# Conv, Fourier mixing, attention and routed block on one core: keys in two halves around the channel DFT, counts behind the second up product, batch 0's first taps on ScalarE, another order in the drain

## The chip, the cores and the metric

The kernel runs on one core of one Trainium2 chip. The metric is the time of one launch in device microseconds. The core has a tensor engine (TensorE, PE in the profile; its weight loads are PEld), VectorE (DVE), ScalarE (ACT), GpSimd (POOL) and SyncE (SP), which here only issues transfers. Each engine works through its own list of instructions in order; semaphores tie the lists together.

## The reference, cut to what matters

The input x has 8 batches of 750 frames with 192 channels. Per batch:

```python
h = depthwise_conv(x, 7 taps) + b_dw            # 750 frames, 192 channels
h = relu(w_pw @ h + b_pw); h = max over pairs   # 375 tokens, 192 channels
y = real(fft2(h))                               # DFT over tokens, then over channels
h = layernorm(y) * gamma + beta                 # "spectrum"
h = h + token_statistics_attention(layernorm(h))     # w_qkv, softmax over tokens, w_out
z = layernorm(h); n = layernorm(z) * g1 + b1
scores = sigmoid(n @ Wr + br)                   # the 56 tokens with the lowest scores
attn = softmax attention (12 heads) for these tokens; mix = (n + scores * pooled) @ Wm + bm
hh = z + where(selected, attn @ Wo + bo, mix)
out = h + hh + gelu(layernorm(hh) @ W1 + bf1) @ W2 + bf2
```

## The kernel before

**Three batches in flight.** Each engine has a function `step(p, q, r, w)`, and `pipeline` calls it in the same order on all of them: batch p in front (convolution, both DFTs, first attention), batch q in the middle (routing and second attention), batch r last (the up and down products of the forward block), and w is the batch whose depthwise sums are made ahead. The steps are (0, -, -), called alone; (1, 0, -), the second step; six full steps from (2, 1, 0) to (7, 6, 5); the drain (-, 7, 6); and the forward block of batch 7 by itself. The order inside a step is written out by hand for each engine, so where an instruction stands in one engine's `step` decides what waits behind it.

**Front batch.** `depthwise` multiplies the frames by a tap and adds: tap 0 on ScalarE (`first_tap`, L893), taps 1 to 6 on VectorE (L390). Batch 0 has a function of its own, `depthwise_first`: for each third of the frames (250) VectorE makes all seven taps for both halves of the channels (L403 for tap 0, L411 for the others), and TensorE's `pointwise` (L1161, L1162) starts on a third when its sums are there. Then `relu` (ACT L884) and `pool_pairs` (DVE L427), `over_tokens` (PE L1171, the DFT over the tokens), `spectrum_parts` (ACT), `over_channels` (PE L1183, the DFT over the channels; it waits for the values' copies and for `block_mix`, DVE L606), `spectrum_stats` (DVE L440), `spectrum_center`, a power on GpSimd (L834), `spectrum_norm`, a second power, `second_norm` (DVE L471, it makes xh), and `front_input` (PE L1119, transposes of xh), behind which the qkv products run.

**Middle batch.** `routed_input` transposes nr (PE L1112) into two banks of `zb`; ScalarE and VectorE split the result into nT (L952, L590). `values_keys` (PE L1127) makes values and scores, and then the keys in two halves, one into bank 3 and one into bank 2 of `zb`; ScalarE copies each to kT (L967). `score_sums` (PE L1268) spreads the scores over the partitions in bank 3, once the first half of kT is copied. VectorE's `ranks` (from L614) compares them, `ranks` on TensorE (L1275, "the counts") sums the comparisons, `slots` on VectorE (L629) makes putT, `slots` on TensorE (L1283) turns it, and `selected`, `selected_queries` (L1301) and `logits` follow. `unselected_scores` (DVE L634) writes one more row of putT. `third_norm` and `third_norm_end` (DVE L569, L576) make nr; L576 waits for a power on GpSimd.

**Last batch.** `forward_input` transposes n2 (PE L1119) and VectorE's `forward_input` (L477, L478) makes the low parts of n2T. `forward_up(r, j)` makes six up products (L1134 to L1142), two banks in turn, so that from the third on each waits for a gelu of ScalarE (L1026). ScalarE loads the Gelu table ahead of them (`table_hint`, L1044) and the Exp table behind them (L1070).

`idle_products` (PE L1409) are products that nobody reads. A product of plain fp32 operands shows as two matmul passes in the trace. On TensorE the order of the part that matters is

```python
                if last:
                    forward_up(r, 0)
                if drain:
                    pe.wait_ge(*h1_done.of(q))
                    idle_products(xb[:, 0], 3)
                if middle:
                    routed_input(q)
                if front:
                    over_tokens(p)
```

and then `values_keys`, `score_sums`, `over_channels`, up products 1 and 2, `ranks`, up product 3, `slots`, up product 4, `selected`, up product 5, `selected_queries`, `front_input`. In the second step idle products stand where the up products do.

## Time and profile before

| what | value |
|---|---|
| three runs | 561.88, 563.33, 565.0 us; median 563.33 us |
| profiled execution, its own time | 564.93 us |
| its span, first to last instruction | 563.1 us |
| mean granted TensorE clock | 0.97 of full |
| busy: TensorE | 500.4 us, 89% of the span |
| busy: VectorE, ScalarE, GpSimd | 430.4 us (76%), 245.5 us (44%), 68.6 us (12%) |
| from one full step to the next (transposes of xh, 282.00 to 342.68) | 60.7 us |

The profiled execution took 1.6 us longer than the median. Times inside the trace count from its first instruction. The busy time of an engine says little by itself: TensorE waits in some places and runs at half its clock in others, so the chain, the waits in brackets in the timeline and the granted clock by window are read together.

### The profile page before, as it was taken

What the parts mean: (1) busy time and instruction counts of PE and PEld (TensorE: products, weight loads), DVE (VectorE), ACT (ScalarE), POOL (GpSimd) and SP (SyncE); (2) the same over time, 40 slices, a digit from 0 to 9 for tenths busy, and PEclk for the clock granted to TensorE, in tenths of its full rate; (3) what the DMA queues carried; (4) which work ended last, traced back from release to release, by engine and by line L of the source; (5) the groups of instructions that cost most, each with busy time, mean ns of one, the idle gap of its engine ahead of it and who ended that gap; (6) DMA issues with size and microseconds to landing.
All of it is one profiled execution on the core that took longest, in us unless ns stands there. A gap on an engine that the chain in (4) does not pass through costs nothing.

```text
span 563.1 us, 9011 instructions
## 1 busy us (share of the span) xinstructions
PE 500.4 (89%) x3066; PEld 412.5 (73%) x3066; DVE 430.4 (76%) x1266; ACT 245.5 (44%) x625; POOL 68.6 (12%) x67
## 2 busy tenths in 40 slices
PE   1588799889989998999999998999899989978786
PEld 1456478659877987788877896798778887857575
DVE  5777869779978997889878998899788574864350
ACT  0244123542666155814673257426571367214721
POOL 0001011101220122001300121012200130012001
PEclk9998999899999998999989999999899998978998
DMA  8350100010001000100001000100000000000001
GB/s 243 114 149 1 41 2 1 1 42 1 1 2 41 17 6 1 42 2 20 0 0 41 20 0 0 41 20 0 0 0 2 20 0 1 2 21 0 2 11 31
DMA packets 8392, 13.26 MB, mean 24 GB/s; under 512 B 1911, under 2 KB 6834, under 8 KB 8365
## 3 DMA queue, kind: packets, MB, share of 16 engines
q1 hardware_dynamic: 8365, 12.92, 8.2%
q8 instruction: 15, 0.25, 0.2%
q14 instruction: 12, 0.10, 0.1%
HBM read 10.61 MB, written 2.30 MB: 23 GB/s over the span
## 4 chain that ended last, share of the span: by engine, by line
PE 64%; DVE 17%; issue 9%; ACT 5%; POOL 3%; DMA 1%; DVEq 0%; SPq 0%; ACTq 0%; POOLq 0%
PE xb L1231 7%; PE xb L1171 6%; PE zb L1127 6%; PE yb L1393 6%; PE xb L1183 3%; POOL rs L834 3%; PE zb L1333 3%; DVE dw L411 2%; PE zb L1341 2%; PE xb L1161 2%; PE xb L1134 2%; ACT w_sq L931 2%; PE xb L1162 2%; PE xb L1222 2%; DVE junk L532 2%
## 5 line engine op out<-in xcount | busy, mean ns | idle before, releaser
L834 POOL TENSOR_TENSOR rs<-ve,half 125x3 f32<-125x3 f32 (+1 forms) x32 | 33.5, 1047 | 375.6 <-DVE ve L378 315.8
L390 DVE SCALAR_TENSOR_TENSOR dw<-x_in,w_dw_sb,dw 96x750 f32<-96x750 f32 x84 | 78.8, 992 | 0.4
L1231 PE MATMUL xb<-scratch,w_sq 128*125 128x192 f32 x288 | 48.8, 327 | 0.8 <-DVE scratch L549 0.7
L1231 PEld LDWEIGHTS xb<-scratch,w_sq 128*125 128x125 f32 x288 | 46.7, 188 | 2.2 <-DVE scratch L549 1.2
L1393 PE MATMUL yb<-w_sb,gelu 128*125 128x192 f32 x252 | 46.2, 326 | 0.0
L1393 PEld LDWEIGHTS yb<-w_sb,gelu 128*125 128x125 f32 x252 | 41.5, 187 | 0.0
L1171 PE MATMUL xb<-dft_n_sb,pooled_h 125*96 125x376 f32 x96 | 34.6, 514 | 1.0 <-DVE pooled_h L427 0.9
L1020 ACT ACTIVATE n2T<-zb 128x375 fp32r<-128x375 f32 (+1 forms) x16 | 7.7, 481 | 61.1 <-PE zb L1119 60.9
L1026 ACT ACTIVATE gelu<-yb,b_sb 128x375 f32<-128x375 f32 x48 | 27.2, 569 | 11.6 <-PE yb L1142 10.6
L1161 PE MATMUL xb<-w_pw_sb,dw 97*125 97x192 f32 x64 | 18.0, 366 | 14.7 <-DVE dw L411 14.0
L1333 PEld LDWEIGHTS zb<-ident_sb,probs 128*125 128x125 f32 x144 | 19.0, 187 | 14.2 <-issue 10.2
L524 DVE TENSOR_TENSOR w_sq<-w_s,xb 128x376 f32<-128x376 f32 x48 | 25.0, 536 | 5.6 <-PE xb L1222 5.6
L930 ACT ACTIVATE w_s<-xb 128x375 f32<-128x375 f32 x48 | 23.9, 499 | 11.8 <-PE xb L1142 11.8
L1333 PE MATMUL zb<-ident_sb,probs 128*125 128x128 f32 x144 | 24.1, 293 | 5.4 <-ACT probsT L1003 2.8
L1171 PEld LDWEIGHTS xb<-dft_n_sb,pooled_h 125*96 125x96 f32 x96 | 16.0, 173 | 16.1 <-issue 15.0
L1134 PE MATMUL yb<-n2T,w_sb 128*128 128x376 f32 x48 | 20.6, 430 | 5.6 <-DVE n2T L478 3.6
L532 DVE CUSTOM_DVE_ANT_0 junk<-w_sq,w_s 128x375 f32<-128x375 f32 x48 | 25.4, 542 | 0.0
L1134 PE MATMUL xb<-xhT,w_qkv_sb 128*128 128x376 f32 x48 | 21.8, 454 | 3.6 <-ACT w_sq L931 2.9
L942 ACT ACTIVATE scratch<-w_out_sb,natt 128x192 f32<-128x192 f32 x24 | 9.2, 445 | 36.3 <-DVE natt L543 36.3
L1003 ACT ACTIVATE probsT<-zb 125x384 f32<-125x384 f32 x48 | 22.2, 493 | 5.7 <-PE zb L1333 5.7
L1161 PEld LDWEIGHTS xb<-w_pw_sb,dw 97*125 97x125 f32 x64 | 11.9, 209 | 16.7 <-issue 12.7
L931 ACT ACTIVATE w_sq<-xb 128x375 f32<-128x375 f32 x48 | 23.9, 499 | 0.0
(215 smaller groups left out, 1284.4 us busy)
## 6 DMA issues: line engine op xcount, KB each, us to landing
x_in<-in_x SPq DMA_DIRECT2D x8, 567.0 KB, 4.2
out<-res_f SPq DMA_DIRECT2D x7, 281.2 KB
gelu<-in_w_qkv SPq DMA_DIRECT2D x1, 768.0 KB, 6.8
gelu<-in_w SPq DMA_DIRECT2D x1, 768.0 KB, 4.3
w_out_sb<-in_w_out SPq DMA_DIRECT2D x1, 576.0 KB
w_sb<-in_w SPq DMA_DIRECT2D x1, 576.0 KB
rows_sb<-in_rows SPq DMA_DIRECT2D x1, 504.0 KB
dft_n_sb<-in_dft_n SPq DMA_DIRECT2D x1, 493.5 KB
```

The costliest lines, as they stand in the source:

```text
L390: dve.scalar_tensor_tensor(out=dw[0:C, c, :], in0=x_in[:, c, k:k + S], scalar=w_dw[:, c, k:k + 1], in1=dw[0:C, c, :], op0=ALU.mult, op1=AL ...
L532: dve.tensor_tensor_reduce(out=junk[:, j % 2, 0:N], in0=u[:, j, 0:N], in1=w_s[:, j, 0:N], scale=1.0, scalar=0.0, op0=ALU.mult, op1=ALU.add ...
L834: pool.tensor_tensor(out_[:], in_[:], half3[:] if len(in_.shape) == 3 else half3[:, 0, :], ALU.pow).then_inc(rs.sem, 1)
L931: act.activation(w_sq[:, j, 0:N], xb[:, j % 2, 0:N], ACT.Square, accum_out=nrm[:, j:j + 1]).then_inc(sq_done.sem, 1)
L1026: act.activation(gelu[:, j, 0:N], yb[:, j % 2, 0:N], ACT.Gelu, bias=b_1[:, j:j + 1]).then_inc(gelu_done.sem, 1)
L1127: ins = mm(o, a[:, k], b[:, l], start=start and k + l == 0, stop=stop and k == 1)
L1134: mm(o, w[:, 0, cols], x[:, 0, :], start=True, stop=False)
L1161: mm(o, dw[0:C + 1, 0, f0:f0 + 2 * P - 1:2], w_pw[:, 0, :], start=True, stop=False)
L1171: ins = mm(xb[0:C, c, 0:2 * KF], pooled_h[:, t, chan(c)], dft_n[:, t, :], start=(t == 0), stop=(t == T - 1))
L1231: ins = mm(o, u[:, j, tok(t)], w_oa[:, j, :], start=(j == 0), stop=(j == IT - 1))
L1333: ins = pe.transpose(zb[0:P, 2 + j % 2, 128 * t:128 * t + 128], probs[:, j, tok(t)], ident[:])
L1393: ins = mm(o, gelu[:, j, tok(t)], w_2[:, j, :], start=(j == 0), stop=(j == IT - 1))
```

## The change

Five things are moved; no arithmetic is changed.

1. Batch 0's tap 0 goes from VectorE (L403) to ScalarE (`first_taps`), third by third, with a semaphore of its own for the first two thirds.
2. `values_keys` is split into `joined_values` and `keys(b, k)`. Both halves of the keys use bank 2, so the second waits for the copy of the first. On TensorE the order becomes values, first half, `score_sums`, `over_channels`, second half. On ScalarE the second copy to kT stands behind the table hint and `spectrum_sines`, ahead of the gelus.
3. Up product 2 goes from before the counts (`ranks`) to behind them.
4. `unselected_scores` on VectorE goes from behind `front_input` to before `second_norm`.
5. In the last full step VectorE runs `third_norm_end` ahead of `forward_input`. In the drain TensorE runs five idle products in place of three, first of all, and up product 0 goes behind `routed_input`.

```diff
@@ -175,7 +175,7 @@
         pads, highs, lows = signal("pads"), signal("highs"), signal("lows")
         dw_first, dw_done = signal("dw_first", CT), signal("dw_done", CT * (K - 1))
-        dw_part = signal("dw_part", CT * K * (T - 1))
+        dw_part, dw_begun = signal("dw_part", CT * (K - 1) * (T - 1)), signal("dw_begun", CT * (T - 1))
         pw_ready, relu_done, pool_done = signal("pw_ready", T), signal("relu_done", T), signal("pool_done", T)
@@ -395,22 +395,18 @@
                 for t in range(T):
                     last = t == T - 1
+                    sem, base = (dw_done.sem, 0) if last else (dw_part.sem, CT * (K - 1) * t)
                     f0, f1 = 2 * P * t, 2 * P * (t + 1)
-                    for k in range(K):
+                    for k in range(1, K):
                         for c in range(CT):
-                            src, dst = x_in[:, c, k + f0:k + f1], dw[0:C, c, f0:f1]
-                            if k == 0:
-                                ins = dve.tensor_scalar(dst, src, w_dw[:, c, 0:1], w_dw[:, c, K:K + 1], ALU.mult, ALU.add)
+                            if k > 1:
+                                dve.wait_ge(sem, base + CT * (k - 2) + c + 1)
+                            elif last:
+                                dve.wait_ge(*dw_first.of(0, c + 1))
                             else:
-                                if not last:
-                                    dve.wait_ge(dw_part.sem, CT * K * t + CT * (k - 1) + c + 1)
-                                elif k == 1:
-                                    dve.wait_ge(*dw_first.of(0, c + 1))
-                                else:
-                                    dve.wait_ge(*dw_done.of(0, CT * (k - 2) + c + 1))
-                                ins = dve.scalar_tensor_tensor(out=dst, in0=src, scalar=w_dw[:, c, k:k + 1], in1=dst,
-                                                               op0=ALU.mult, op1=ALU.add)
-                            ins.then_inc((dw_first if k == 0 else dw_done).sem if last else dw_part.sem, 1)
+                                dve.wait_ge(dw_begun.sem, CT * t + c + 1)
+                            dve.scalar_tensor_tensor(out=dw[0:C, c, f0:f1], in0=x_in[:, c, k + f0:k + f1], scalar=w_dw[:, c, k:k + 1],
+                                                     in1=dw[0:C, c, f0:f1], op0=ALU.mult, op1=ALU.add).then_inc(sem, 1)
 
@@ -753,14 +749,14 @@
                     spectrum_center(p)
                     spectrum_norm(p)
+                if middle:
+                    unselected_scores(q)
                 if front:
...
                 if front:
                     front_input(p)
-                if middle:
-                    unselected_scores(q)
                 if first(p):
@@ -805,11 +801,13 @@
                 if front:
                     third_norm(p)
+                if ends(p):
+                    third_norm_end(p)
                 if middle:
...
                 if last and middle and not front:
                     result(r, 1)
-                if front:
+                if front and not ends(p):
                     third_norm_end(p)
@@ -893,6 +891,16 @@
                        .then_inc(dw_first.sem, 1)
 
+            def first_taps():
+
+                act.wait_ge(taps_in.sem, 16)
+                act.wait_ge(*x_ready.of(0))
+                for t in range(T):
+                    f0, f1 = 2 * P * t, 2 * P * (t + 1)
+                    for c in range(CT):
+                        act.activation(dw[0:C, c, f0:f1], x_in[:, c, f0:f1], ACT.Identity, scale=w_dw[:, c, 0:1], bias=w_dw[:, c, K:K + 1])\
+                           .then_inc((dw_first if t == T - 1 else dw_begun).sem, 1)
+
             def split_high(k):
@@ -951,7 +959,7 @@
                 act.activation(nT[0:C, 0, :, 0:N], zb[0:C, 0:2, 0:N], ACT.Copy).then_inc(nT_high.sem, 1)
 
-            def values_keys(b):
+            def joined_values(b):
                 for k, (t0, t1) in enumerate(((0, 2), (2, 3))):
@@ -962,9 +970,10 @@
                     src = zb[0:P, 0:2, 0:D] if k == 0 else joined(2)[:, 0:D].unsqueeze(1)
                     act.activation(v[:, t0:t1, :], src, ACT.Copy).then_inc(v_done.sem, 1)
-                for c in range(CT):
-                    act.wait_ge(*k_ready.of(b, c + 1))
-                    act.activation(kT[:, c, 0:N], zb[0:C, 3 - c, 0:N], ACT.Identity, bias=b_k[:, c:c + 1]).then_inc(kT_done.sem, 1)
+
+            def keys(b, c):
+                act.wait_ge(*k_ready.of(b, c + 1))
+                act.activation(kT[:, c, 0:N], zb[0:C, 2, 0:N], ACT.Identity, bias=b_k[:, c:c + 1]).then_inc(kT_done.sem, 1)
 
@@ -1038,12 +1047,15 @@
                     spectrum_parts(p)
                 if middle:
-                    values_keys(q)
+                    joined_values(q)
+                    keys(q, 0)
 
...
                 if front:
                     spectrum_sines(p)
+                if middle:
+                    keys(q, 1)
                 if first(p):
@@ -1100,6 +1112,7 @@
                     forward_input(q)
 
+            first_taps()
             pipeline(act, step)
@@ -1149,7 +1162,7 @@
                     if first(b):
                         if t < T - 1:
-                            pe.wait_ge(dw_part.sem, CT * K * (t + 1))
+                            pe.wait_ge(dw_part.sem, CT * (K - 1) * (t + 1))
                         else:
@@ -1238,7 +1251,7 @@
                 transposes(nr, zb).then_inc(nT_ready.sem, 1)
 
-            def values_keys(b, p):
+            def joined_values(b, p):
                 if first(b):
@@ -1255,14 +1268,16 @@
                     if t:
                         ins.then_inc(v_ready.sem, 1)
-                for k in range(CT):
-                    for c in range(CT):
-                        ins = split_product(zb[0:C, 3 - k, 0:NE], w_k[:, :, c, chan(k)], nT[0:C, :, c, :], c == 0, c == 1)
-                    ins.then_inc(k_ready.sem, 1)
+
+            def keys(b, k):
+                if k:
+                    pe.wait_ge(*kT_done.of(b, 1))
+                for c in range(CT):
+                    ins = split_product(zb[0:C, 2, 0:NE], w_k[:, :, c, chan(k)], nT[0:C, :, c, :], c == 0, c == 1)
+                ins.then_inc(k_ready.sem, 1)
 
             def score_sums(b):
 
-                pe.wait_ge(*kT_done.of(b, 1))
                 pe.wait_ge(*sc_steps.of(b, 2))
@@ -1416,31 +1431,35 @@
                 if front:
                     pointwise(p, q)
-                if last:
+                if last and front:
                     forward_up(r, 0)
                 if drain:
                     pe.wait_ge(*h1_done.of(q))
-                    idle_products(xb[:, 0], 3)
+                    idle_products(xb[:, 0], 5)
                 if middle:
                     routed_input(q)
+                if drain:
+                    forward_up(r, 0)
                 if front:
                     over_tokens(p)
                 if middle:
-                    values_keys(q, p)
-                if middle:
+                    joined_values(q, p)
+                    keys(q, 0)
                     score_sums(q)
                 if front:
                     over_channels(p, q)
+                if middle:
+                    keys(q, 1)
                 if alone:
...
                 if last:
                     forward_up(r, 1)
-                    forward_up(r, 2)
                 if second:
...
                     ranks(q)
                 if last:
+                    forward_up(r, 2)
                     forward_up(r, 3)
```

## Rows read from the trace of the kernel before

**Rows 1.** The page, part 4: the chain that ended last, shares of the span by engine

```profile
PE 64%; DVE 17%; issue 9%; ACT 5%; POOL 3%; DMA 1%; DVEq 0%; SPq 0%; ACTq 0%; POOLq 0%
```

**Rows 2.** Timeline of the first 30 us: start us, us, engine line op out<-in xcount [idle before <-releaser]

```profile
6.09 0.72 DVE L403 TENSOR_SCALAR dw<-x_in,w_dw_sb 96x250 f32<-96x250 f32 x2 [5.01 <-DMA x_in<-in_x]
...
22.17 1.00 PE L1161 MATMUL zb<-w_pw_sb,dw 97*125 97x192 f32 x2 [2.39 <-DVE dw L411]
...
27.37 1.92 ACT L893 ACTIVATE dw<-x_in,w_dw_sb 96x750 f32<-96x750 f32 x2 [0.53 <-issue]
```

**Rows 3.** Timeline of one full step, 264 to 276 us

```profile
264.40 2.56 PE L1127 MATMUL zb<-w_vm_sb,nT 97*125 97x386 f32 x12
...
267.86 2.21 PE L1127 MATMUL zb<-nT,w_k_sb 96*96 96x376 f32 x12
...
269.12 0.35 DVE L606 TENSOR_TENSOR zed<-xb,zed 125x192 f32<-125x192 f32 x1
...
269.91 0.49 PE L1268 MATMUL zb<-ident_sb,nr 125*125 125x125 f32 x3
...
270.23 2.76 PE L1183 MATMUL xb<-dft_d_sb,scratch 96*125 96x97 f32 x24
...
270.43 0.86 DVE L614 SCALAR_TENSOR_TENSOR less<-zb,nr,later_sb 125x125 bf16<-125x125 f32 x3 [0.96 <-PE zb L1268]
...
270.69 1.28 ACT L1044 ACT_TABLE_LOAD   x1
...
272.77 0.42 PE L1134 MATMUL yb<-n2T,w_sb 128*128 128x376 f32 x1
...
274.58 0.64 PE L1275 MATMUL zb<-less,ones_bf 125*65 125x375 bf16 x3
...
275.26 0.60 DVE L629 TENSOR_SCALAR putT<-zb,slot_sb 64x375 f32<-64x375 f32 x1 [0.28 <-PE zb L1275]
```

**Rows 4.** Timeline of the same step, 280 to 285 us

```profile
280.89 0.96 DVE L471 TENSOR_SCALAR even<-res,ag,rs 125x192 f32<-125x192 f32 x3 [0.96 <-POOL rs L834]
...
282.00 0.51 PE L1119 MATMUL xb<-ident_sb,even 125*128 125x125 f32 x3 [1.52 <-DVE even L471]
...
284.62 0.55 DVE L634 SCALAR_TENSOR_TENSOR putT<-zb,score_row 1x375 f32<-1x375 f32 x1
```

**Rows 5.** Transposes of xh two steps and one step earlier; then a window (PEclk is last but two)

```profile
162.05 0.51 PE L1119 MATMUL xb<-ident_sb,even 125*128 125x125 f32 x3 [1.52 <-DVE even L471]
...
221.15 0.51 PE L1119 MATMUL xb<-ident_sb,even 125*128 125x125 f32 x3 [1.52 <-DVE even L471]
...
284.00:285.00 1.00, 1.00 (x5) 0.81 (x4) 0.94 (x3) 0.00 (x0) 0.00 (x0) 0.50 0.00 0
```

**Rows 6.** Timeline of the second step, 90 to 95 us

```profile
90.12 2.76 PE L1183 MATMUL xb<-dft_d_sb,scratch 96*125 96x97 f32 x24
...
92.72 1.45 PE L1409 MATMUL yb<-dft_n_sb 125*125 125x376 f32 x4
...
94.78 0.58 DVE L629 TENSOR_SCALAR putT<-zb,slot_sb 64x375 f32<-64x375 f32 x1
```

**Rows 7.** Timeline of the drain, 498 to 521 us

```profile
498.06 1.42 POOL L834 TENSOR_TENSOR rs<-ve,half 125x6 f32<-125x6 f32 x1 [4.19 <-DVE ve L565]
...
500.03 1.08 DVE L576 SCALAR_TENSOR_TENSOR nr<-nr,rs,rows_sb 125x192 f32<-125x192 f32 x3
...
500.06 0.68 PE L1134 MATMUL yb<-n2T,w_sb 128*128 128x376 f32 x1 [3.59 <-DVE n2T L478]
...
501.79 3.83 PE L1409 MATMUL xb<-dft_n_sb 125*125 125x376 f32 x6
...
505.46 0.80 PE L1112 MATMUL zb<-ident_sb,nr 125*96 125x125 f32 x6
...
508.11 3.69 PE L1127 MATMUL zb<-w_vm_sb,nT 97*125 97x386 f32 x12 [1.85 <-DVE nT L590]
...
520.17 0.85 PE L1283 MATMUL zb<-ident_sb,putT 64*125 64x64 f32 x6
```

## The prediction

> **What bounds the kernel now.** The page comes first: TensorE is the busiest engine, and the chain that ended last lies on it for 64% of the span, on VectorE for 17% [rows 1]. So time is won where TensorE stands still or runs slowly, and where another engine holds up the ends of the run, which nothing covers. The chain and the timeline of a full step (three batches in flight) show one such place: TensorE is idle for 1.52 us before the transposes of xh, released by VectorE's L471 at 282.00 [rows 4]. That stall is the end of a serial chain on VectorE and GpSimd: ranks, putT (L629), spectrum_center, power, spectrum_norm, power, L471, which itself waited 0.96 us for GpSimd [rows 4]. The windows view then shows what follows the stall: TensorE's granted clock is 0.50 in 284 to 285, which is 1.2 GHz [rows 5]. It fell behind this stall in four of the six full steps (not in those whose transposes start at 162 and 343). The price is read from the starts of the transposes: 162.05 to 221.15 is 59.10 us (a step whose first part ran at 2.4 GHz), 221.15 to 282.00 is 60.85 us [rows 4, 5]. I take 1.6 us as the price of one slow step. Last, the two ends: in the first 22 us VectorE alone makes batch 0's depthwise sums [rows 2], and in the drain TensorE runs an up product and idle products, at half clock, in front of transposes whose input is long there [rows 7].
>
> **First taps.** VectorE loses three pairs of L403, 0.72 us a pair [rows 2]; the next op started 0.64 us after each pair's start. Now ScalarE makes them, which has nothing to do before the first pointwise product. Two of its 96x750 taps took 1.92 us [rows 2], so some 1.0 us each. For 96x250 the bounds are a third (0.33) and the whole (1.0); I take 0.58, nearer the third, since part of an instruction is fixed. VectorE's first accumulation then starts at 6.09 + 0.58 + 0.05 = 6.72, as it does now, and the second waits about 0.1 for the other tap. The later two thirds find their taps done, so 2 x 0.64 - 0.1 = 1.2 us are gained (1.4 with the low bound, 0.5 with the high). The last pointwise product, at 22.17 behind L411, is the path [rows 2], and all behind it moves along; the loads for batch 1, the weights and w_1 are issued behind the last sum on SP and move with it. The Trainium skill ("ScalarE: Activation LUTs", Rules for kernel authors) says to use VectorE, not ScalarE, for add and mul. By that rule alone the six taps would cost more; the trace agrees that one tap is cheaper on VectorE (0.4 against my 0.58), but here it is taken off the only busy engine.
>
> **The full step.** Today TensorE makes both halves of the keys from 267.86, the score sums (L1268) at 269.91, the channel DFT (L1183) at 270.23, two up products from 272.77, and the counts (L1275) at 274.58 [rows 3]. One half of the keys is 1.02 us, one up product 0.905 us (half of 274.58 - 272.77). New order:
> - score sums after one half: 268.89, 1.02 us earlier. VectorE has waited 0.96 us for them before L614 [rows 3]; it is free at 269.47 (second L606), so the ranks start 0.9 earlier.
> - channel DFT: would start at 269.21, but it waits for L606: 269.12 + 0.35 + 0.06 = 269.53 [rows 3]. TensorE loses 0.3 here, and the DFT is 0.70 earlier.
> - second half of the keys at 269.53 + 2.54 = 272.07. It reuses the bank that ScalarE emptied long before.
> - first up product 273.09, counts 274.00: 0.58 earlier. They also wait for kT's second half on ScalarE: keys end 273.25, plus 0.57 and 0.1 is 273.92. The slack is under 0.1.
> - putT (L629) waits for the counts: 0.58 earlier, and behind it on VectorE spectrum_center and the whole chain to L471. VectorE itself could be 0.9 earlier; the counts bind, so 0.58 is the term. Bounds: 0.9, and 0 if the kT copy or a gelu is later than worked out.
> - ScalarE's queue now holds gelu 0 and 1 behind the second kT copy. Gelu 0 ends near 274.32, the third up product wants it at 274.35: nothing lost, again by a hair. Up to 0.9 of delay here would be hidden by the stall before the transposes.
> - unselected_scores (0.55 us, L634 at 284.62 [rows 4]) goes into the 0.96 us wait before L471 and costs nothing; without that cover it would cost 0.55. Its removal behind L478 gains nothing either: the exponentials are paced by ScalarE, where squares come first.
>
> TensorE's work up to the stall is unchanged but for the 0.3 us wait, of which some 0.2 is got back where it now waits before slots. So the transposes come 0.58 earlier and the stall shrinks from 1.5 to about 0.9. Six full steps: -3.5 us (bounds 0 and -5.4).
>
> **The second step** (batch 1 in front, no third batch) has two idle products in place of the up products, and they stay ahead of the counts. The DFT starts at 90.12 today [rows 6] and at 89.49 then; half the keys and the idle products follow (2.60 for the DFT, 1.02, and 1.29 for four passes of some 0.32, [rows 6]), so the counts come at 94.40 against 94.0 and L629 at 95.08 against 94.78 [rows 6]: +0.3 us.
>
> **The drain.** Today: up product 500.06, idle products 501.79, transposes of nr 505.46, values 508.11 [rows 7]. Then: VectorE finishes nr first. GpSimd's power ends at 498.06 + 1.42 = 499.48, L576 takes 1.08 (to 500.6), the two low parts of n2T follow to 501.7. The five idle products start when h1 is there, near 496.5, behind other transposes (today TensorE's wait of 3.59 us begins there [rows 7]), while the clock is still up: 10 passes of 0.32 are 3.2 us [rows 6]. The transposes still wait for n2T of the batch before (same bank), so they start at 501.75, 3.7 us earlier, and the values at 504.4. From the values on, 12.06 us pass until slots at 520.17 [rows 7], of which about 1.6 are half clock (their first twelve products took 3.69, against 2.56 in a full step [rows 3, 7]). The score sums lose 1.02 in front of them, two up products come behind the counts. I get slots at about 514.7 at full clock (-5.5) and 516.4 with today's clock (-3.8); I take -5.0. Only the serial attention of batch 7 follows, and moves along.
>
> **Sum.** -1.2 + 0.3 - 3.5 - 5.0 = -9.4 us. The profiled execution took 564.93 us (span 563.1), 1.60 above the median of 563.33; the three runs differ by 1.45 and 1.67, near one slow step each, so I read the median as three slow steps where the profile has four (an estimate). A stall of 0.9 in place of 1.5 should let the clock fall less often. No row shows how often; the bounds are none and three of three spared (0 and -4.9), and I take one, -1.6. 563.33 - 9.4 - 1.6 = 552.3 us; from the profile, with four slow steps turned into two, 564.93 - 9.4 - 3.2 = 552.3.
>
> **Rivals.**
> - *Only the ends gain.* The two slacks under 0.1 on ScalarE are negative, the counts start no earlier, the clock falls as before: 563.33 - 1.2 + 0.3 - 5.0 = 557.4. For it: the kT copy and gelu 0 now queue behind a product that TensorE makes late. Against it: each is worked out from rows of the same operations.
> - *The clock stays up in every step*: 563.33 - 9.4 - 4.9 = 549.0. For it: it stayed up in two of six behind the longer stall.
> - *Table reloads make it slower.* The second kT copy (Identity) now stands behind the Gelu table load (1.28 us [rows 3]). If Identity needed another table, a load stands before it and one after: gelu 0 ends near 276.9, the third up product is 2.6 late, slots at 278.7, the queries end near 283.1, past the 282.0 of the transposes: +1.1 a step. It decides from about 1.5 us of delay. With the clock down in all six (+4.9) and 2 us less in the drain: 563.33 - 0.9 + 6.6 + 4.9 - 3.0 = 570.9. Against it: the page's list and the timeline have one load for each hint, and Copy runs under Gelu's table with none.
> - *Gains lost on the way* (drain half, steps nothing, second step more): 560.5 to 566, no change.
>
> The Trainium skill ("ScalarE: Activation LUTs", Table sets: the hidden batching unit) says that cheap functions such as relu, copy and identity are in every table set. By that rule the reload rival gives no load at all; the trace agrees for Copy, and shows Identity only under the Exp table.
>
> **Chances.** The forecast 0.60 (own range 549 to 556); only the ends 0.17; clock up throughout 0.12; no change 0.06; slower 0.05. What a measurement here can tell from no change is 0.5%, 2.8 us: faster means under 560.5. So faster 0.89, same 0.06, slower 0.05. The range takes in both neighbours: 547.5 to 558.5.
>
> **What would show it.** L1161's last product near 21.0 in place of 22.17; L614 with no wait; L629 0.58 earlier against L1127 than now; TensorE's stall before L1119 near 0.9; fewer stretches at clock 0.50; L629 of the second step 0.3 later; in the drain L1409 from 496.5 on at 0.32 a pass and L1112 released by VectorE's L478. The prediction is wrong if gelu 0 or the kT copy releases TensorE in each step, if a table load stands before L967, or if the clock falls in the drain before the values.

## The result and the profile after

The changed kernel took 556.16 us (median of 4 runs, 555.98 to 556.78) against 563.82 (4 runs, 561.88 to 565.0) for the kernel before: ratio 0.9869 [0.9839, 0.9899]. The time is inside the range, and the sign is the predicted one; it is 3.9 us above the point. A later set of six runs gave 553.27 (552.76 to 553.8, and one disturbed run at 709.19 that the range and the ratio leave out) against 563.97: ratio 0.9803 [0.9739, 0.9867]. The two sets differ by 2.9 us, and that is a finding of its own (see the clock, below).

The profiled execution took 556.28 us, its span is 554.5 us (563.1 before), its mean granted clock 0.981 (0.970 before). From the page, the clock in 40 slices, then the shares of the chain that ended last:

```profile
PEclk9979899799999999999999999999999999999899
...
PE 62%; DVE 17%; issue 11%; ACT 5%; POOL 3%; DMA 1%; ACTq 0%; SPq 0%; DVEq 0%; POOLq 0%
```

TensorE carries 62% of the chain in place of 64% [rows 1]. The slices of the full steps all read 9; the low ones are now in the first 110 us and in the drain.

Timeline of the first 30 us after (it answers to [rows 2]):

```profile
6.27 1.28 ACT L901 ACT_TABLE_LOAD   x1 [6.27 <-DMA x_in<-in_x]
7.57 3.03 ACT L901 ACTIVATE dw<-x_in,w_dw_sb 96x250 f32<-96x250 f32 x6
8.31 14.11 DVE L408 SCALAR_TENSOR_TENSOR dw<-x_in,w_dw_sb,dw 96x250 f32<-96x250 f32 x36 [7.24 <-ACT dw L901]
...
22.48 1.00 PE L1174 MATMUL zb<-w_pw_sb,dw 97*125 97x192 f32 x2 [1.75 <-DVE dw L408]
```

The last pointwise product starts 0.31 us later than before, not 1.2 earlier. ScalarE's first activation carries a table load of 1.28 us, and it stands behind the wait for x. VectorE starts at 8.31 where 6.72 was forecast. In the kernel before, the same load ran at the very start, where it cost nothing; the activation it belongs to ran at 14.56:

```profile
0.74 1.28 ACT L884 ACT_TABLE_LOAD   x1 [0.74 <-PEq L1618]
14.56 0.33 ACT L884 ACTIVATE even<-xb 125x192 f32<-125x192 f32 x1 [12.54 <-PE xb L1162]
```

Timeline of the full step that [rows 3, 4] show, after. Its products begin 1.55 us later in this profile (256.78 against 255.23), so 1.55 comes off each start before it is compared:

```profile
265.95 2.56 PE L1140 MATMUL zb<-w_vm_sb,nT 97*125 97x386 f32 x12
...
270.43 0.49 PE L1283 MATMUL zb<-ident_sb,nr 125*125 125x125 f32 x3
...
270.96 0.86 DVE L610 SCALAR_TENSOR_TENSOR less<-zb,nr,later_sb 125x125 bf16<-125x125 f32 x3
...
271.17 2.83 PE L1196 MATMUL xb<-dft_d_sb,scratch 96*125 96x97 f32 x24 [0.25 <-DVE zed L602]
...
275.06 0.57 ACT L976 ACTIVATE kT<-zb,b_k_sb 96x375 f32<-96x375 f32 x1 [1.92 <-PE zb L1140]
275.53 1.02 ACT L1035 ACTIVATE gelu<-yb,b_sb 128x375 f32<-128x375 f32 x2
...
275.72 0.64 PE L1290 MATMUL zb<-less,ones_bf 125*65 125x375 bf16 x3
...
276.40 0.60 DVE L625 TENSOR_SCALAR putT<-zb,slot_sb 64x375 f32<-64x375 f32 x1 [0.63 <-PE zb L1290]
...
282.03 0.96 DVE L467 TENSOR_SCALAR even<-res,ag,rs 125x192 f32<-125x192 f32 x3 [0.39 <-POOL rs L832]
...
283.13 0.51 PE L1132 MATMUL xb<-ident_sb,even 125*128 125x125 f32 x3 [0.60 <-DVE even L467]
```

Score sums at 268.88 (forecast 268.89), channel DFT 269.62 (269.53), counts 274.17 (274.00), putT 274.85 against 275.26: 0.41 earlier, where 0.58 was forecast. VectorE's 0.96 us wait for the score sums is gone, and it waits 0.63 for the counts instead. The transposes are 0.42 earlier and the stall before them is 0.60 in place of 1.52.

The windows view behind that stall (it answers to [rows 5]; PEclk is last but two), and two stretches where the clock is at half in this execution:

```profile
284.00:285.00 1.00, 1.00 (x8) 0.45 (x9) 0.40 (x1) 0.90 (x3) 0.46 (x1) 1.00 0.00 0
...
36.00:42.00 6.00, 6.00 (x23) 4.82 (x23) 2.12 (x11) 3.02 (x5) 0.00 (x0) 0.50 0.05 19
...
524.00:525.00 1.00, 1.00 (x20) 0.94 (x15) 0.00 (x0) 0.20 (x1) 0.00 (x0) 0.50 0.00 0
```

Second step (it answers to [rows 6]) and drain (to [rows 7]), timeline:

```profile
86.58 2.56 PE L1140 MATMUL zb<-w_vm_sb,nT 97*125 97x386 f32 x12
...
97.50 0.60 DVE L625 TENSOR_SCALAR putT<-zb,slot_sb 64x375 f32<-64x375 f32 x1 [0.95 <-PE zb L1290]
...
492.08 3.42 PE L1424 MATMUL xb<-dft_n_sb 125*125 125x376 f32 x10
...
497.36 0.82 PE L1125 MATMUL zb<-ident_sb,nr 125*96 125x125 f32 x6 [1.86 <-DVE n2T L474]
...
500.03 2.40 PE L1140 MATMUL zb<-w_vm_sb,nT 97*125 97x386 f32 x12 [0.99 <-DVE nT L586]
...
510.27 0.86 PE L1298 MATMUL zb<-ident_sb,putT 64*125 64x64 f32 x6
...
523.60 2.76 PE L1356 MATMUL zb<-probsT,v 125*32 125x128 f32 x36
```

In the second step putT comes 10.92 us behind the values' first product, 10.50 before (the product at 84.28): +0.42, forecast +0.3. In the drain the idle products run at 0.34 a pass, not 0.64, and the slots' transposes come at 510.27 in place of 520.17.

Where the 8.6 us between the two profiled spans are (starts in us; the steps are marked by the transposes of xh, the drain by the transposes of n):

| point | before | after | gained in the stretch that ends here |
|---|---|---|---|
| last pointwise product, batch 0 | 22.17 | 22.48 | -0.31 |
| second step's transposes | 101.41 | 104.15 | -2.43 (0.4 order, the rest clock) |
| first full step's transposes | 162.05 | 165.60 | -0.81 (+0.4 step, -1.2 clock) |
| drain, transposes of n | 495.66 | 491.24 | +7.97 |
| drain, values | 508.11 | 500.03 | +3.66 |
| drain, slots | 520.17 | 510.27 | +1.82 |
| end of the span | 563.1 | 554.5 | -1.30 (clock) |

Two mechanisms sit in the 7.97. A period is the time from one full step's transposes of xh to the next step's. Before, periods were 59.10, 60.85, 60.68, 59.23 and 60.86 us: three of them, and the stretch into the drain, hold a slow 3 us each. After, they are 58.70, 58.83, 58.83, 58.83 and 58.95. The two undisturbed ones, the first and the fourth, fell by 0.40 each, which is 2.0 in five. What is left of the five periods' 6.6 is 4.6 for the three slow stretches (1.5 each), and the stretch into the drain, with the fourth, gave 1.4: 6.0 of clock.

### The profile page after: what moved, and what is told of

It reads as the page before. It is cut to its first block, busy times and chain, and to the rows that moved or that the text cites. A ratio compares the mean times of both kernels' runs of the same rounds, so it can differ in the third digit from the quotient of the medians.

```text
span 554.5 us, 9016 instructions
## 1 busy us (share of the span) xinstructions
PE 499.6 (90%) x3070; PEld 409.8 (74%) x3070; DVE 429.4 (77%) x1260; ACT 248.4 (45%) x631; POOL 68.5 (12%) x67
## 4 chain that ended last, share of the span: by engine, by line
PE 62%; DVE 17%; issue 11%; ACT 5%; POOL 3%; DMA 1%; ACTq 0%; SPq 0%; DVEq 0%; POOLq 0%
PE xb L1244 7%; PE yb L1408 6%; PE xb L1184 5%; PE xb L1196 4%; PE zb L1140 4%; POOL rs L832 3%; PE zb L1348 3%; DVE dw L408 3%; DVE dw L390 2%; PE zb L1424 2%; PE zb L1356 2%; PE xb L1174 2%; PE xb L1235 2%; PE xb L1175 2%; PE xb L1224 1%
## 5 line engine op out<-in xcount | busy, mean ns | idle before, releaser
L1196 PE MATMUL xb<-dft_d_sb,scratch 96*125 96x97 f32 x192 | 24.6, 289 | 3.6 <-DVE zed L602 1.9
L1196 PEld LDWEIGHTS xb<-dft_d_sb,scratch 96*125 96x125 f32 x192 | 23.4, 202 | 5.4 <-issue 3.1
```

The source lines that it names most:

```text
L1196: ins = mm(xb[0:P, r, KL * t:KL * t + KL], f[:, c, tok(t)], dft_d[:, r, c, :], start=(c == 0), stop=(c == 1))
```

## The experiments

Each label's ratio is against the kernel before, measured beside it. "Idle products" are products whose result nobody reads; they add work and leave none out. No experiment leaves out part of the computation.

| run | us, median (range) | ratio [95%] |
|---|---|---|
| early_table | 555.15 (550.75-555.71) | 0.9788 [0.9738, 0.9839] |
| taps_on_vector | 553.70 (553.09-555.71) | 0.9789 [0.9745, 0.9833] |
| old_drain | 559.26 (556.17-560.38) | 0.9867 [0.9817, 0.9916] |
| filled_stall | 560.5 (558.57-566.78) | 0.9935 [0.9895, 0.9976] |
| changed_again | 553.27 (552.76-553.8) | 0.9803 [0.9739, 0.9867] |
| second_up_ahead | 568.97 (567.12-571.55) | 1.0075 [1.0039, 1.011] |
| scores_late | 555.12 (552.38-557.12) | 0.983 [0.9768, 0.9892] |
| filled_ends | 548.70 (548.54-550.78) | 0.973 [0.9672, 0.9787] |
| ends_vector_taps | 549.79 (548.97-550.96) | 0.9721 [0.9678, 0.9763] |
| ends_scores_late | 548.94 (548.46-550.86) | 0.9717 [0.9673, 0.9761] |
| ends_whole_keys | 551.63 (549.02-555.29) | 0.9739 [0.9693, 0.9785] |
| before_filled | 552.28 (551.32-555.39) | 0.9769 [0.9724, 0.9814] |

The first four were measured together, then the next four, then the last four, each time on another chip; the kernel before had medians of 564.99, 563.97 and 565.54 beside them. So a median is compared safely only inside its set of four; across sets the starts in the profiles carry the argument.

**early_table: an activation of one element ahead of the wait for x.** On the changed kernel:

```
                 act.wait_ge(taps_in.sem, 16)
+                act.activation(table_hint[:], w_dw[0:1, 0, 0:1], ACT.Identity)
                 act.wait_ge(*x_ready.of(0))
```

> The changed kernel with one tiny Identity on ScalarE behind the wait for the taps, so that the table load (1.28 us, now at 6.27, behind the arrival of x) runs while x is still in flight. Theory A (the load behind the wait ate the gain of the first taps): VectorE's first accumulation starts near 6.8 in place of 8.31, the last pointwise product near 21.0 in place of 22.48, and the time falls by 1.5 us, from 556.2 to about 554.7. Theory B (the start is not on the path, the clock of TensorE in the first 100 us decides): the product moves, but the time stays within 0.5 us of 556.2 or goes either way by up to 2.

Its timeline:

```profile
0.74 1.28 ACT L897 ACT_TABLE_LOAD   x1 [0.74 <-PEq L1638]
...
6.11 2.06 ACT L902 ACTIVATE dw<-x_in,w_dw_sb 96x250 f32<-96x250 f32 x4 [3.56 <-DMA x_in<-in_x]
...
6.85 1.26 DVE L408 SCALAR_TENSOR_TENSOR dw<-x_in,w_dw_sb,dw 96x250 f32<-96x250 f32 x3 [5.78 <-ACT dw L902]
...
21.02 1.00 PE L1175 MATMUL zb<-w_pw_sb,dw 97*125 97x192 f32 x2 [1.76 <-DVE dw L408]
```

The load leaves the path, and the last pointwise product starts at 21.02, 1.46 earlier than after the change and where the prediction had put it (near 21.0). In the median the gain does not show clearly (555.15 against 556.16): the profile has the clock at half in 514 to 523 and 527 to 530, and the spread of its runs is 5 us.

**taps_on_vector: batch 0's first tap back on VectorE.**

```
-                    for k in range(1, K):
+                    for k in range(K):
...
+                            if k == 0:
+                                dve.tensor_scalar(dw[0:C, c, f0:f1], x_in[:, c, f0:f1], w_dw[:, c, 0:1], w_dw[:, c, K:K + 1],
+                                                  ALU.mult, ALU.add).then_inc((dw_first if last else dw_begun).sem, 1)
+                                continue
...
-            first_taps()
```

> The changed kernel with batch 0's first taps back on VectorE. Theory A (moving them cost 0.3 us net, as the last pointwise product went from 22.17 to 22.48): 555.9 us, 0.3 below the changed kernel. Theory B (moving them gained what I forecast and something else was lost in the start): 557.4, 1.2 above.

The last pointwise product starts at 22.43 against 22.48 for the changed kernel; counted from the landing of x it is 16.08 (x at 6.35) against 16.21 (x at 6.27). As written, the new taps bring nothing. The median is under both forecasts: 2.5 us under the first set of the changed kernel, and level with its second (553.27). Its profile lacks the slow stretch at 35 to 42 us, and its transposes of the first full step start 3.5 earlier (162.12 against 165.60), so that gap is clock.

**old_drain: VectorE's and TensorE's order in the drain as before, the rest changed.**

```
-                if ends(p):
-                    third_norm_end(p)
...
-                if front and not ends(p):
+                if front:
                     third_norm_end(p)
...
-                if last and front:
+                if last:
                     forward_up(r, 0)
...
-                    idle_products(xb[:, 0], 5)
+                    idle_products(xb[:, 0], 3)
...
-                if drain:
-                    forward_up(r, 0)
```

> The changed kernel with the drain's order and the end of the last full step as before. Theory A (the new order is worth the 3.7 us by which the values start earlier plus the half clock it spares, less what the clock takes later): 4 to 5.5 us slower than the changed kernel, 560.2 to 561.7. Theory B (most of the drain's gain is the keys and counts, not the order ahead of the values): 1 to 2 us slower, 557 to 558.

Timeline, values' first product:

```profile
502.69 2.56 PE L1138 MATMUL zb<-w_vm_sb,nT 97*125 97x386 f32 x8 [1.85 <-DVE nT L586]
```

It comes 11.58 us behind the transposes of n (491.11); in the changed kernel 8.79 (491.24 to 500.03). The slots come at 514.43, 4.2 later than 510.27, and the span is 2.9 longer (557.4 against 554.5), since the changed kernel loses some of it again at half clock in 523 to 526. That is between the two forecasts. The medians, 559.26 against 556.16, say 3.1 (the runs spread over 4.2).

**filled_stall: on the kernel before, two idle products in the stall of [rows 4].**

```
                     pe.wait_ge(*gelu_done.of(r))
+                    idle_products(yb[:, 1], 2)
                 pe.wait_ge(*xh_done.of(b))
```

> The kernel before, with two idle products in TensorE's stall of 1.52 us before the transposes of xh (four passes of 0.32, 1.3 us, so they fit into the stall). No other work is moved. Theory A (what the shorter stall gives in the changed kernel is mostly the clock, which falls behind the stall): the granted clock stays full in all full steps, each period is 59.1 us, and with three or four slow steps at 1.65 us spared the time is 557.5 to 559, 1% below before. Theory B (the clock falls for another reason, or the order of the work gives the gain): 563 to 565, no change, or slower by up to 0.2 us a step where the idle products run past the stall.

Its timeline:

```profile
281.92 1.53 PE L1410 MATMUL yb<-dft_n_sb 125*125 125x376 f32 x4
...
283.33 0.54 PE L1119 MATMUL xb<-ident_sb,even 125*128 125x125 f32 x3
```

With nothing else changed, all full periods are 59.06 to 59.20 and the clock is 1.00 in each. Five of them sum to 295.86 us against 300.72 before: 4.9 us won by work that nobody reads. So theory A holds of the steps. The whole run gained less than it said (median 560.5, ratio 0.9935): the profile shows more half clock at the ends, in 35 to 41, 103 to 110, 496 to 502 and some shorter stretches behind them.

**changed_again: the changed kernel once more, unedited.**

> The changed kernel once more, beside the kernels of this call. Both theories: 555.5 to 557, with all full steps at 2.4 GHz and periods near 58.8 us. If some of its runs come out by 3 us or more lower or higher, the clock in the first and last 100 us decides that, not the change.

The median is 2.2 us under the forecast. Periods as in the first profile (58.69 to 58.90), but no half clock in 35 to 42 (3 us in 46 to 49 instead): second step's transposes at 101.02 in place of 104.15. Of the 3.4 us between the two spans (554.5 and 551.1), 3.1 arise ahead of them.

**second_up_ahead: keys still in halves, the third up product's place undone** (`forward_up(r, 2)` back in front of the counts).

> The changed kernel with the up product 2 ahead of the counts again, so that the keys in halves stand alone. Theory A (the chain to xh starts with the counts, on TensorE): the counts and putT come 0.88 us later in each full step, TensorE's stall before the transposes grows from 0.6 to about 1.4, the period from 58.8 to about 59.7, and the clock falls again in some steps: 5 to 9 us slower than the changed kernel, 561 to 565. Theory B (the earlier DFT over the channels is what counts, the counts are hidden): within 1 us of it.

Timeline:

```profile
277.96 0.57 ACT L976 ACTIVATE kT<-zb,b_k_sb 96x375 f32<-96x375 f32 x1 [1.92 <-PE zb L1140]
278.43 1.02 ACT L1035 ACTIVATE gelu<-yb,b_sb 128x375 f32<-128x375 f32 x2
...
279.04 0.44 PE L1147 MATMUL yb<-n2T,w_sb 128*128 128x376 f32 x1 [0.26 <-ACT gelu L1035]
...
280.01 0.64 PE L1290 MATMUL zb<-less,ones_bf 125*65 125x375 bf16 x3
...
280.69 0.60 DVE L625 TENSOR_SCALAR putT<-zb,slot_sb 64x375 f32<-64x375 f32 x1 [2.02 <-PE zb L1290]
...
287.42 0.51 PE L1132 MATMUL xb<-ident_sb,even 125*128 125x125 f32 x3 [1.52 <-DVE even L467]
```

Worse than either forecast, and slower than the kernel before. Gelu 0 stands in ScalarE's queue behind the second kT copy, which waits for a product that TensorE now makes late; the next up product waits for gelu 0 (its bank), and the counts stand behind that. The stall is 1.52 again, the one undisturbed period is 60.24 (before 59.23, changed 58.83), and the others are 61.50 to 61.83.

**scores_late: unselected_scores back behind front_input.**

> The changed kernel with unselected_scores behind front_input on VectorE again. Theory A (0.55 us inside a wait for GpSimd, nobody waits for what it was moved away from): within 0.5 us of the changed kernel, L467's wait back at 0.96 in place of 0.39, same period of 58.8. Theory B (its new place gives a share of the gain, since the maxima come 0.55 earlier): periods of 59.2 to 59.4, 2 to 3 us slower.

Periods 58.66 to 58.91 as in the changed kernel, with L467's wait back at 0.96, as theory A said. Against 553.27, measured beside it, the median is 1.9 higher with overlapping ranges, and the profile has the slow stretch at 35 to 42 again; the step itself shows no difference. ends_scores_late, below, settles it.

**filled_ends: the changed kernel with the stalls at the two ends filled.** It has early_table's line, the second step's counts ahead of its two idle products, and more idle products: two where TensorE waits in the second step, and three single ones, as below, in the drain (the expectation says four; the edit has three, and the trace shows them at 510.18, 513.59 and 518.75).

```
                 if second:
-                    idle_products(yb[:, 0], 2)
                 if middle:
                     ranks(q)
+                if second:
+                    idle_products(yb[:, 0], 2)
...
+                if second:
+                    idle_products(yb[:, 0], 2)
                 if front:
                     front_input(p, r)
...
+                if drain:
+                    idle_products(xb[:, 0], 1)
```

> The changed kernel with the early table load, the second step's counts ahead of its two idle products, two more idle products before the transposes of xh in the second step, and four single idle products in the stalls of the drain's attention. Theory A (what is left of the difference between runs is the clock at the two ends): the granted clock stays full from 110 us to the end but for stretches before the last forward block, and the time is 549 to 552, 4 to 6 us below the changed kernel, with less spread. Theory B (the idle products lengthen the drain's serial chain as much as the clock gives): 554 to 557.

From its page, and the window that answers to 36 to 42 above:

```profile
PEclk9999999999999999999999999999999999999999
```

```profile
36.00:42.00 6.00, 6.00 (x21) 3.57 (x20) 5.52 (x24) 1.76 (x2) 0.89 (x1) 1.00 0.01 1
```

548.70 us, the best version: 15.3 us below the kernel before and 4.6 below the changed kernel measured beside it. Last pointwise product at 20.96, periods 58.71 to 58.87, mean clock 0.999.

The next three undo one part each on this quieter base, and the fourth puts the filling on the old order.

**ends_vector_taps** (taps as in taps_on_vector).

> The kernel of filled_ends (548.7 us, clock full nearly throughout, so small edits can be told apart) with batch 0's first taps back on VectorE. Theory A (with the table loaded in time the taps on ScalarE are worth 2 x 0.64 less a wait): 1.2 to 1.5 us slower, 549.9 to 550.2, the last pointwise product near 22.3. Theory B (hidden by something later in the first batch): within 0.3 us of 548.7.

Last pointwise product at 22.15 against 20.96 (x landed at 6.06 and 6.04): the first taps are worth 1.2 us once the table load is out of the way. The median is 1.1 higher, though across two sets.

**ends_scores_late** (order as in scores_late).

> The kernel of filled_ends with unselected_scores behind front_input again. Theory A (worth nothing at either place): within 0.3 us of 548.7, periods 58.8. Theory B: 0.5 us a step, 3 us slower.

548.94 against 548.70, with periods of 58.68 to 58.90: nothing, as the prediction priced it.

**ends_whole_keys** (both halves of the keys before the score sums, in two banks, both kT copies behind them; the up product's new place kept).

```
                     keys(q, 0)
+                    keys(q, 1)
                     score_sums(q)
...
                     over_channels(p, q)
-                if middle:
-                    keys(q, 1)
```

> The kernel of filled_ends with both halves of the keys ahead of the score sums, as before the change, and the up product 2 still behind the counts. Theory A (the counts alone do most of it; they would then be ready at about 0.9 us before their old time, but VectorE reaches putT only behind spectrum_stats, 0.25 us before its old time against 0.41 for the halves): periods of 59.0, 0.16 us a step above filled_ends, about 1 us slower in all. Theory B (the halves are what starts the chain earlier, 0.4 us a step or more): periods of 59.2, 2.4 us or more slower.

Periods 58.85, with halves 58.84 (both forecasts said 59.0 or more). Timeline of whole keys, then of filled_ends:

```profile
262.06 2.57 PE L1140 MATMUL zb<-w_vm_sb,nT 97*125 97x386 f32 x12
...
268.11 0.86 DVE L610 SCALAR_TENSOR_TENSOR less<-zb,nr,later_sb 125x125 bf16<-125x125 f32 x3 [0.96 <-PE zb L1282]
...
271.40 0.64 PE L1289 MATMUL zb<-less,ones_bf 125*65 125x375 bf16 x3
...
272.56 0.58 DVE L625 TENSOR_SCALAR putT<-zb,slot_sb 64x375 f32<-64x375 f32 x1
...
279.28 0.51 PE L1132 MATMUL xb<-ident_sb,even 125*128 125x125 f32 x3 [1.12 <-DVE even L467]
```

```profile
259.36 2.57 PE L1141 MATMUL zb<-w_vm_sb,nT 97*125 97x386 f32 x12
...
269.14 0.64 PE L1291 MATMUL zb<-less,ones_bf 125*65 125x375 bf16 x3
...
269.82 0.60 DVE L625 TENSOR_SCALAR putT<-zb,slot_sb 64x375 f32<-64x375 f32 x1 [0.62 <-PE zb L1291]
```

Behind the values' first product, the counts come at 9.34 (whole) and 9.78 (halves), putT at 10.50 and 10.46; before, they were 10.18 and 10.86 [rows 3]. With whole keys VectorE is the late one: it waits 0.96 for the score sums and then has no idle time up to putT. With halves TensorE is: VectorE waits 0.62 for the counts. The two come out within 0.04 us. TensorE's stall before the transposes is 1.12 us with whole keys and 0.61 with halves, at the same period, and the clock stayed at 1.00 in all full steps behind either. The median is 2.9 higher, with the lowest run at 549.02 against 548.54; its profile is at half clock in 35 to 41 and 506 to 512.

**before_filled** (the kernel before with filled_stall's idle products, those of the ends, and in the drain five idle products ahead of the first up product on TensorE, as in the change; VectorE's orders, keys, counts and taps as before).

> The kernel before with idle products only: two in the stall of each full step, two more in the second step, five in place of three at the head of the drain with the up product 0 behind them, four single ones in the drain's attention. Keys, counts, first taps and VectorE's order stay as before. Theory A (most of the difference between the kernels is TensorE's clock): periods of 59.2, clock full almost throughout, 553 to 556 us, that is as fast as the changed kernel or 1 to 2 us faster. Theory B (the new order is most of the gain): 559 or more.

(It too has three single products in the attention, not four.) 552.28 against 565.54: -13.3 us, without one step of the new order outside TensorE's drain. Full periods of 59.03 to 59.18; filled_ends has 58.71 to 58.87. Between them lie 3.6 us: 1.9 at the start (22.86 to 20.96, of which 0.73 only because x landed at 6.77 instead of 6.04) and some 0.32 a step.

## Why the prediction was right or wrong

**In sum.** -9.4 for the edits and -1.6 for the clock were forecast; the profile shows -8.6 in all, the two sets of medians -7.7 and -10.7. Counted from the profile (564.93 - 9.4 - 3.2 = 552.3), the changed kernel's profiled execution, 556.28, is 4.0 above. The first taps make 1.5 of that, the full steps 1.1, the clock 1.7 and the second step 0.1; the drain gives 0.5 back. The time is inside the range because the range is wide. That the second set comes within 1.0 of the point is luck: the clock fell less at the ends there, which no term of the sum had foreseen.

**First taps, -1.2: wrong, measured +0.3** by the profile (0.18 of it since x landed at 6.27 and not 6.09). The step that failed is "VectorE's first accumulation then starts at 6.09 + 0.58 + 0.05 = 6.72". It left out the table load of ScalarE's first activation, which ran at 0.74 before and now stands behind the wait for x. The rest of the step holds: a tap takes 0.51 (3.03 for six) against the forecast 0.58 and VectorE's 0.36 (half of 0.72), and with the load moved the gain is 1.15 (22.17 to 21.02), with 1.2 between the starts of ends_vector_taps and filled_ends (22.15 and 20.96).

**The full step, -0.58 each: right in mechanism, too large; measured -0.40** of undisturbed period (59.10 to 58.70 and 59.23 to 58.83), 2.4 us in six steps instead of 3.5; between before_filled and filled_ends it is 0.31 to 0.34. The starts up to the DFT were right within 0.1. The counts came 0.41 earlier instead of 0.58: the DFT and the second half of the keys took 0.1 longer together, and the slack "under 0.1" between kT's copy and the counts was gone (in filled_ends the copy ends at 269.06 and the counts' first weights load at 269.11). TensorE also got to the transposes 0.50 later than before (at 280.98, with the 1.55 taken off, against 280.48): its wait ahead of the DFT cost 0.4, and nothing of it was got back before the slots, where the forecast had 0.2. So the stall shrank to 0.6, not 0.9. What I had not seen is which edit pays. ends_whole_keys has the same period without the halves; second_up_ahead has the halves without the moved product and loses 1.0 a step against the kernel before (60.24 to 59.23). The gain of 0.3 to 0.4 belongs to the up product behind the counts. The halves take away VectorE's wait and give TensorE an equal delay.

**Clock, -1.6 on the median and -3.2 on the profile: near in sum, by two misses that cancel.** I took one slow step of three as spared (two of the profile's four); the profile after has none in any full step: four spared, 6.0 us between these two profiles. filled_stall shows that the stall alone did it: same order, stall filled, no slow step, 4.9 us in five periods. Against that, the sum had put the clock at the ends at nothing, and 3.2 us were lost to it up to the first full step and 1.3 in the drain's attention, where the changed profile is at half clock and before was not, or less long. The clock's net is -1.5. The ends differ from run to run: changed_again had no slow 35 to 42 and was 2.9 us quicker. So the rival "the clock stays up in every step" (549.0) was right of the steps and wrong of the run.

**Second step, +0.3: right**, measured +0.42.

**Drain, -5.0: right up to the slots, less at the end.** Transposes of n to slots fell from 24.51 to 19.03 us, 5.5, which is the forecast at full clock. Of it 4.3 is the drain's order, with the half clock that the old one brings in 496 to 499 and 503 to 506: old_drain, with the keys in halves, takes 23.32. At the end of the span 2.9 of it are left, as the attention behind it fell to half clock. In VectorE's order the nr-first part earns nothing that the runs show: before_filled, with nr last, has its transposes of nr 5.50 us behind those of n, filled_ends with nr first 6.11. In filled_ends they wait 1.86 for VectorE's n2T (L474), which now stands behind nr; in before_filled nr itself (L576) releases them. That order was not tried by itself.

**Rivals.** Only the ends gain (557.4): refuted, the counts come earlier and the periods fall, though its time is 1.2 from the first median. Table reloads: refuted, kT's second copy (L976 at 275.06) runs between the Gelu load at 271.21 and gelu 0 with no load of its own. The Trainium skill ("ScalarE: Activation LUTs", Table sets: the hidden batching unit) says that identity is in every table set. This trace agrees, for Identity under Gelu's table, which the trace of before did not show. *Gains lost on the way* (560.5 to 566): refuted by both sets. Unselected_scores at nothing: right, by two runs.

**Left open.** What makes the clock fall at 35 to 42 in some executions: it did in six of these profiles and in eight it did not; the changed kernel, unedited, shows it once and once not. The last pointwise product lies at 20.9 to 22.8 in those without it and at 21.7 to 22.9 in those with it, so its time alone does not decide. Nor does the chip: of each later set of four, on a chip of its own, some profiles show the stretch and some do not. Also open is why one table load stands behind the waits of its activation and the others ahead of them (see the last section).

## What to carry to other kernels

A TensorE stall of 1.5 us on the path can cost as much again in the clock behind it; fill it with unread products before reordering anything, for that is one line and was worth 4.9 us over five steps here (4.5 in the median of the whole). When work moves to an engine that was idle, ask what its first instruction drags along (a table load) and which wait that then stands behind. When an order is changed to relieve one engine, look at what waits in the queues of the others, and at who is late next: both can make a correct saving worth nothing.

## What the runs showed of the hardware

Where the table load of ScalarE's first activation lands depends on what that activation is. It ran at 0.74 us in the kernel before, though its activation (behind one wait, for TensorE) ran at 14.56, and at 0.74 in early_table, though the one-element activation then waited for the taps until 2.35. It ran only at 6.27, behind the arrival of x, where the first activation stands behind two waits (taps and x). It is 1.28 us long each time, and in the last case the next activation starts at once behind it (7.57). What decides between the two places, no run shows.

A stall of 0.60 us in front of the transposes left the clock at 1.00 in every full step, and so did one of 1.12 in ends_whole_keys; one of 1.52 was followed by 3 us at 0.50 in four of the steps before, and in five of six in second_up_ahead.

Unread products are worth more than the change under study: 13.3 us of 565.5 in before_filled, where the kernel before has a mean clock of 0.970, which looks like little. Some 3 of the 13.3 may be the drain's order on TensorE, which before_filled shares with the change (old_drain undoes it, with VectorE's order there, for 3.1).
